# New work lists for VectorE and ScalarE, tile 13 by eight products, and the addition of x1 on GpSimd instead of in a DMA

## The reference, cut to what matters

```python
def block1(x):                       # on LN(x), _layernorm without weights
    uv = x @ in_proj_w + in_proj_b   # 512 -> 1024
    u, v = uv[..., :512], silu(uv[..., 512:])
    v = depthwise_conv3(v) + conv_b  # along the rows (time)
    h_t = a * h_{t-1} + ssm_b * v_t; y_t = ssm_c * h_t + ssm_d * v_t
    out = (u * silu(y)) @ out_proj_w + out_proj_b
    return layernorm_with_weights(out + x)

def ffn(x):                          # on LN(x1)
    h = gelu(x @ ternary(W1).T + b1) # 512 -> 2048
    return h @ ternary(W2).T + b2    # 2048 -> 512

x1  = x  + LN(block1(LN(x)))
out = x1 + LN(ffn(LN(x1)))
```

## Time and profile before

| | us |
|---|---|
| three runs: median (lowest to highest) | 1498.55 (1497.08 to 1499.59) |
| the profiled execution's own time | 1498.6 |
| its span, first to last instruction | 1496.8 |
| PE busy in the span | 1416.4 (95%) |
| DVE busy | 1220.6 (82%) |
| ACT busy | 913.1 (61%) |
| POOL busy | 356.5 (24%) |

### The profile page before, as it was taken

One profiled execution on the slowest core, in us unless ns is written; L12 is line 12 of the kernel. 1 busy time (PEld: TensorE's weight loads), 2 busy tenths in 40 slices (PEclk: granted clock), 3 DMA queues, 4 the chain that ended last, 5 costly groups with the idle time before them and its releaser, 6 DMA issues.

```text
span 1496.8 us, 25048 instructions
## 1 busy us (share of the span) xinstructions
PE 1416.4 (95%) x9002; PEld 885.7 (59%) x9002; DVE 1220.6 (82%) x2402; ACT 913.1 (61%) x1504; POOL 356.5 (24%) x522
## 2 busy tenths in 40 slices
PE   7999999899999999999999999999999999989997
PEld 4444646457475664756657566574666747555664
DVE  7999869788797887978889698897988879898634
ACT  7997756556466564674756556575665646743543
POOL 4243321222202222131222212222122220222111
PEclk9999999999999999999999999999999999999999
DMA  8702613215122151320513304142131512202320
GB/s 248 259 30 58 166 31 76 38 29 113 29 63 51 29 113 29 85 43 15 113 28 87 55 13 103 29 100 42 44 71 29 113 29 58 29 1 57 57 29 29
DMA packets 164653, 98.13 MB, mean 66 GB/s; under 512 B 133680, under 2 KB 133680, under 8 KB 164400
## 3 DMA queue, kind: packets, MB, share of 16 engines
q1 hardware_dynamic: 155888, 80.79, 21.2%
q0 software_dynamic: 8640, 15.73, 7.4%
HBM read 31.49 MB, written 32.51 MB: 43 GB/s over the span
## 4 chain that ended last, share of the span: by engine, by line
PE 37%; DVE 30%; issue 15%; ACT 8%; POOL 3%; DVEq 0%; POOLq 0%; ACTq 0%
PE f1b L614 6%; PE f1b L613 6%; DVE bn L904 5%; PE f2b L664 4%; DVE ring L922 3%; PE misc L576 3%; PE misc L578 3%; PE misc L577 3%; PE f2b L654 3%; ACT tp L1944 3%; ACT xn L1934 2%; DVE hb L1161 2%; PE f2b L639 2%; PE f2b L637 2%; POOL rsc L2278 2%
## 5 line engine op out<-in xcount | busy, mean ns | idle before, releaser
L613 PE MATMUL f1b<-x3T,w 128*128 128x256 f16 x1792 | 400.7, 274 | 0.0
L614 PE MATMUL f1b<-x3T,w 128*128 128x256 f16 x1792 | 400.5, 274 | 0.0
L1840 ACT ACTIVATE ring<-f1b,par 128x256 f32<-128x256 f32 x480 | 201.1, 470 | 237.3 <-PE f1b L614 237.0
L2277 POOL TENSOR_SCALAR ve<-mv 128x4 f32<-128x4 f32 (+2 forms) x89 | 36.8, 414 | 797.5 <-DVE mv L914 797.3
L922 DVE SCALAR_TENSOR_TENSOR ring<-ring,f_sc 128x512 f16<-128x512 f32 x256 | 187.3, 738 | 34.8 <-ACT ring L1854 34.8
L654 PE MATMUL f2b<-w,ring 128*128 128x512 fp8e5 x768 | 197.1, 379 | 0.0
L613 PEld LDWEIGHTS f1b<-x3T,w 128*128 128x128 fp8e5 x1792 | 176.2, 98 | 24.8 <-issue 0.4
L614 PEld LDWEIGHTS f1b<-x3T,w 128*128 128x128 fp8e5 x1792 | 176.0, 98 | 24.2
L1854 ACT ACTIVATE ring<-ring,f_sc 128x512 f16<-128x512 f32 x256 | 182.2, 719 | 0.0
L576 PE MATMUL misc<-x1T,win_hi 128*128 128x512 f16 x456 | 179.4, 393 | 0.0
L577 PE MATMUL misc<-x1T,win_hi 128*128 128x512 f16 x456 | 178.6, 392 | 0.0
(11 more groups left out here) (263 smaller groups left out, 2823.4 us busy)
## 6 DMA issues: line engine op xcount, KB each, us to landing
out_dram<-xs SPq DMA_DIRECT2D x60, 256.0 KB, 2.7
xs<-x_dram SPq DMA_DIRECT2D x14, 1024.0 KB, 6.1
out_dram<-hb POOLq DMA_DIRECT2D x36, 256.0 KB, 5.4
out_dram<-stage POOLq DMA_DIRECT2D x24, 256.0 KB, 4.6
ring<-w1t_dram SPq DMA_DIRECT2D x3, 1024.0 KB, 13.1
stage<-w2t_dram SPq DMA_DIRECT2D x3, 1024.0 KB, 8.4
x1T<-tp SPq DMA_TRANSPOSE x68, 3.1
xs<-x_dram SPq DMA_DIRECT2D x4, 256.0 KB, 4.1
```

Source lines behind the costliest of these rows:

```text
L613: pe.matmul(o_, w, src[:, k, h * TH:(h + 1) * TH], start=k == 0, stop=False)
L614: mm = pe.matmul(o_, w, src[:, KC + k, h * TH:(h + 1) * TH], start=False, stop=k == KC - 1)
L1840: ins = act.activation(gg[:, i % G_SLOTS, ts], f1b[i % 2][:, ts], ACT.Gelu, bias=par[:, B1 + chunk:B1 + chunk + 1], scale=1.0 / ACT_SCALE)
```

## The change

1. **Lists of VectorE and ScalarE.** In the first part of a stage: the taps of blocks 2 and 3 stand before the scans; d_conv of blocks 2 and 3 moves from 6.15 and 7.15 to 4.15 and 4.16; ffn_norm of a tile by seven moves from 4.15..5.2 to 6.15..7.2; the statistics of blocks 2 and 3 of the FFN's result (f_stats) move from .8 to 2.27; lo of the sixth unit (5) gets the time 4.2. In the written part h_add(c, 0) stands before the last t_lo, and three operations of `drain` stand between the t_lo. In the second part lo has new times (AT_LO_SECOND).
2. **combine.** Of eight, three are made in the written part of stage 3, and one instead of three at its end.
3. **Tile 13 by eight.** `seven` ends at tile 12. Stage 15's sums, seven-part drains and its statistics in two halves become lo, f_add and statistics of a tile by eight.
4. **The sum with x1.** `finish` is GpSimd's tensor_tensor of two 128 x 512 float32 blocks in SBUF. SyncE stores the result (`store`) and no longer stores x1. `load_x(e+4)` waits for fin_ok, that is for the four additions of tile e, and stands in SyncE's list behind its four stores.

```diff
-AT_TAP0, AT_TAP2 = (1.1, 1.15, 1.4, 1.45), (1.3, 1.35, 2.4, 2.45)
+AT_TAP0, AT_TAP2 = (1.1, 1.15, 1.4, 1.45), (1.3, 1.35, 2.25, 2.26)
-AT_LO = (1.2, 2.2, 2.32, 2.38, 3.36)
-AT_D_CONV, AT_CENTRE = (3.15, 3.16, 6.15, 7.15), (13.3, 13.5, 14.3, 14.5)
+AT_LO = (1.2, 2.2, 2.32, 2.38, 3.36, 4.2)
+AT_D_CONV, AT_CENTRE = (3.15, 3.16, 4.15, 4.16), (13.3, 13.5, 14.3, 14.5)
+AT_LO_SECOND = (9.3, 11.2, 11.65, 13.2, 14.2, 15.2, 16.2)
+AT_F_STATS_SEVEN = 2.27
+AT_F_NORM_SEVEN = (6.15, 6.2, 7.15, 7.2)
-AT_COMBINED = (7.65, 7.66, 11.65, 11.66, 14.65, 17.5, 17.51, 17.52)
+AT_COMBINED = (7.65, 9.25, 11.65, 14.65, 17.5)
@@
     def seven(t):
-        return 1 < t < NT - 2
+        return 1 < t < NT - 3
@@ load_x
                 if t >= X_SLOTS:
-                    sp.wait_ge(n3_ok, NB * (t - X_SLOTS + 1))
-                    for j in range(NB):
-                        sp.wait_ge(x1_st[j], 16 * (t - X_SLOTS + 1))
+                    sp.wait_ge(fin_ok, NB * (t - X_SLOTS + 1))
@@
-            def store_x1(t):
...
+            def store(t, j):
+                if t < NT - 1:
+                    sp.wait_ge(fin_ok, NB * t + j + 1)
+                else:
+                    sp.wait_ge(fin_last, j + 1)
+                sp.dma_start(out_d[t, j], fo(t, j)).then_inc(out_st[j], 16)
@@ SyncE, for each stage s
-                if e is not None and e + X_SLOTS < NT:
-                    load_x(e + X_SLOTS)
-                if s == 3:
-                    store_x1(1)
+                if e is not None:
+                    for j in range(NB):
+                        store(e, j)
+                    if e + X_SLOTS < NT:
+                        load_x(e + X_SLOTS)
@@ VectorE, the written part
+                parts = drain(fa, 0) if seven(fa) else []
                 if n is not None:
-                    for j in range(NB):
-                        t_lo("t1", n, j)
...
+                    t_lo("t1", n, 1)
+                    for part in parts[:3]:
+                        part()
+                    t_lo("t1", n, 2)
+                    h_add(c, 0)
+                    for part in parts[3:4]:
+                        part()
+                    t_lo("t1", n, 3)
+                    parts = parts[4:]
@@ GpSimd
             def finish(e, j):
                 pool.wait_ge(fn_ok, NB * e + j + 1)
-                pool.wait_ge(x1_st[j], 16 * (e + 1))
-                pool.dma_start(out_d[e, j], fo(e, j), accum_op=ALU.add).then_inc(out_st[j], 16)
+                pool.tensor_tensor(fo(e, j), fo(e, j), xs[:, e % X_SLOTS, j, :], ALU.add).then_inc(fin_ok, 1)
```

More of the change, by code:

```diff
@@ L519, in _ @@
                     transposes("t3", c)
-                if c is not None and c < NT - 1:
-                    store_x1(c)
             for j in range(NB):
-                store_last(j)
+                store(NT - 1, j)
             for j in range(NB):
-                sp.wait_ge(x1_st[j], 16 * (NT - 1))
-                sp.wait_ge(out_st[j], 16 * (NT - 1))
-                sp.wait_ge(last_st[j], 16)
+                sp.wait_ge(out_st[j], 16 * NT)
         @block.tensor
@@ L1036, in epilogue @@
                     return (spread(AT_F_ADD, .1, drain(e, 1))
-                            + spread(AT_F_STATS, .1, [lambda j=j: f_stats(e, j) for j in range(2, NB)])
-                            + spread(AT_F_AGGR, .01, [lambda j=j: aggr(4, e, j) for j in range(2, NB)]))
+                            + spread(AT_F_STATS_SEVEN, .001, [lambda j=j: f_stats(e, j) for j in range(2, NB)])
+                            + spread(AT_F_STATS_SEVEN + .004, .001, [lambda j=j: aggr(4, e, j) for j in range(2, NB)]))
                 return (spread(AT_F_ADD, .2, [lambda j=j: f_add(e, j) for j in range(NB)])
@@ L1739, in _ @@
                     gate(c, 1)
+                if s == 3:
+                    combine(2, 0)
                 if n is not None:
@@ L1751, in _ @@
                     gate_lo(c, 3)
+                parts = drain(fa, 0) if seven(fa) else []
                 if n is not None:
-                    for j in range(NB):
-                        t_lo("t1", n, j)
+                    if s == 3:
+                        combine(0, 0)
+                    t_lo("t1", n, 0)
+                    if s == 3:
+                        combine(0, 1)
+                    t_lo("t1", n, 1)
[7 more added lines that the diff above has]
+                    parts = parts[4:]
                 if s == NT - 1:
@@ L1760, in _ @@
                 if c is not None:
-                    parts = drain(fa, 0) if seven(fa) else []
                     for j in range(NB):
-                        h_add(c, j)
-                        for part in parts[2 * j:2 * j + 2]:
-                            part()
+                        if n is None or j > 0:
+                            h_add(c, j)
                         if s == NT - 1:
@@ L1773, in _ @@
                                 aggr(1, c, j - 2)
+                        for part in parts[2 * j - 2:2 * j] if j else []:
+                            part()
                     h_stats(c, NB - 1)
@@ L1783, in _ @@
                 if s == 3:
-                    works = [b2_difference] + [lambda q=q, g=g: combine(q, g) for q in range(4) for g in range(2)]
-                    items += list(zip((AT_COMBINED[0],) + AT_COMBINED, works))
+                    b2_difference()
+                    items += [(at, lambda i=i: combine(*divmod(i, 2))) for i, at in zip((2, 3, 5, 6, 7), AT_COMBINED)]
                 if s < NT - 1:
@@ L1788, in _ @@
                 if fa is not None:
-                    at_lo = AT_LO_LAST if s == NT - 1 else [j + 1.2 for j in range(half(s), FC)]
+                    at_lo = AT_LO_LAST if s == NT - 1 else AT_LO_SECOND
                     items += lows(fa, range(half(s), FC), [0] * half(s) + list(at_lo))
@@ L1804, in _ @@
                     t_lo("t3", NT - 2, 3)
-                    parts = drain(NT - 3, 1)
-                    for part in parts[:4]:
-                        part()
+                    f_add(NT - 3, 0)
+                    f_add(NT - 3, 1)
                     h_add(NT - 1, 0)
-                    for part in parts[4:]:
-                        part()
+                    f_add(NT - 3, 2)
+                    f_add(NT - 3, 3)
                     for j in range(NB):
-                        if j > 1:
-                            f_stats(NT - 3, j)
+                        f_stats(NT - 3, j)
                         if j < NB - 1:
@@ L2215, in _ @@
                 if e is not None:
-                    items += [(at, lambda j=j: ffn_norm(e, j)) for j, at in enumerate(AT_F_NORM)]
+                    items += [(at, lambda j=j: ffn_norm(e, j)) for j, at in enumerate(AT_F_NORM_SEVEN if seven(e) else AT_F_NORM)]
                 if c is not None and s < NT:
```

26 lines of the change are left out of this document (7 added, 19 removed).

## The result

| | before | after |
|---|---|---|
| median of four runs, us | 1498.87 | 1458.83 (1455.72 to 1462.79) |
| ratio, 95% interval | | 0.9736 (0.9711 to 0.9761) |
| the profiled execution: its own time, its span | 1498.6, 1496.8 | 1458.7, 1456.9 |
| PE busy | 1416.4 (95%) | 1400.7 (96%) |
| DVE busy | 1220.6 (82%) | 1263.0 (87%) |

The kernel is 40 us faster, by the profiled executions 39.9. Lines have moved by about eleven: L653 of after is L664 of before, L955 is L966, L911 is L922, L1074 is L1085 and L1130 is L1141.

What follows compares the result with a forecast made beforehand. PE, busy for 95% of the span, was taken as the bound. From 1498.6 us, eleven stages of 89.4 for 91.41 (-22), stage 15 (-8.5) and stage 4's start (-2.3) gave 1465.8, rounded to 1466 us; range 1433 to 1508.

Steps and rivals of the forecast that it cites:

- rival B: All four additions go in one by one ahead of the sums; PE waits 3.1 us, clock always falls: 1480 us, chance 0.15.
- The scan's wait: First part of a stage: with d_conv early, block 3's scan no longer waits; undisturbed, 2.31 us of PE's idle time goes.
- the margin: Sums of units 4 and 5 ready at 557.5 us, 1.5 ahead of PE, of which 1.0 was taken.
- h_add: Placed ahead of the last split, it removes PE's 1.2 us wait in a stage, with 1.0 us to spare.
- The price of an addition: On VectorE ahead of the sums of units 4 and 5: each addition costs 0 or 1.02 us.
- rivals A and C: A: additions cost nothing, 1428 to 1440 us, chance 0.27; C: additions starve, ln1 waits for x, 1500 to 1520, chance 0.17.
- How many get in: Three of four additions go in ahead of the sums of units 4 and 5, so PE waits 2.1 us.
- The clock: Behind the wait for the sums, the clock falls in ten of twelve stages, 1.69 us each.
- The stage without waits: A stage without PE's 4.12 us of waits and the 1.69 us fall would take 85.9 us.
- The end: Tile 13 by eight removes the waits for sums in stage 15: 8.5 us taken, with 0 and 9.9 as ends.
- load_x: It waits for the fourth addition; x lands at 566.3 us, wanted by ln1 at 565.9; the delay is covered.
- The DMAs: The store of x1 and the adding DMAs are gone; no wait of PE rests on them, so nothing is gained.

Runs made afterwards that it cites:

- the multiplications: After, with GpSimd multiplying the block by 1.0 in place of adding x1 in the tiles by seven: 1421.98 us.
- The kernel with three additions: After, with block 3 of the tiles by seven added over 8 of 512 columns only: 1451.82 us.
- the kernels without waits: After with the adding DMA in place of GpSimd's additions, 1415.66 us; after with all additions of tiles by seven cut to 8 columns, 1418.33 us.

## Why the prediction was right, and where it wasn't

The time (1466 predicted, 1458.8 measured) and its sign were right, and so was the mechanism: what PE waited for, what took these waits away, and that each addition delays VectorE ahead of the sums. How many additions get in was wrong, and there rival B, to which the prediction gave 0.15, had it right. That the stage came out at 89.4 us all the same is luck: over eleven stages the fourth addition cost about 10 us more than predicted, the rarer falls 5.5 and the faster stage 4.4 less. The 7 us that are left lie at the end.

*The waits and their causes.* Right. The scan's wait, the margin (1.0 taken, 0.7 to 0.8 measured), h_add (1.2, and 1.2 when it was put back), the start of stage 4 (2.3 taken, 2.4 measured). The second pair of sums had no margin to spare, as was said: without additions its products begin 1.13 us behind the start of the four matmuls ahead of them, elsewhere 0.87.

*The price of an addition.* 1.02 us from stage 15, 0.97 measured. Right, and it was the number on which all depended. The row of 6.48 us, on which rivals A and C rested, wasn't repeated: the longest of the new additions took 2.28 us.

*How many get in.* Wrong: three taken, four came. The step said that the fourth arrives when the sums are nearly through. It placed the sums where an undisturbed VectorE makes them; but three additions had pushed them back by 2.9 us, and the fourth caught the first of them. An addition makes room for the next. The count was that of rival B. The rule of the Trainium skill (page "SBUF — State Buffer", section "SBUF: two separate sides") that stood behind it agrees with these additions: all four went in one by one, and VectorE lost 0.97 us of the 1.27 of each. It doesn't agree with the multiplications, which read SBUF as well and cost VectorE 0.32 us each; there the measurement decides. The kernel with three additions shows the predicted case: a wait of 2.1 us and a fall in most stages.

*The clock.* Wrong: falls in ten of twelve stages taken (1.4 us for a stage), four of nine measured, 0.9 on the average. The price of one was not 1.69 either but 1.6 twice and 2.9 twice. I took it that a wait as long as before, in the same place, brings the fall with it. In the profiled executions it came less often with a wait of 3.0 than with one of 2.1, and in the kernel before with additions behind none of eleven waits of 2.3 us (380 to 1301 us). The largest part of rival B's miss (1480) comes from this too: it counted a fall in each stage, which is 9 of its 21 us; 7 more are the end's and 4 the faster stage's.

*The stage without waits.* 85.9 taken, 85.33 measured. Rows 1 gave the waits of PE as idle time, but PE's busy time was 85.93 there and is 85.24 in the kernels without waits: with the four waits 0.7 us of busy time went too. In after a stage less its wait is 88.52 - 3.02 = 85.5. With 3.0 for 2.1, 0.9 for 1.4 and 85.5 for 85.9 a stage comes to 89.4, the predicted figure.

*The end.* 10.5 taken (2.0 for the last of the eleven stages and 8.5 for tile 13), 17.7 measured. Tile 13 by eight is worth 11.6 alone. Left out was the wait of 1.6 us for h_add in stage 15, and the caution of 1.4 was not needed. The stage ahead of it lost 3.5 us, not 2.0: 0.6 of sums, 1.2 of h_add and 1.69 of a fall of the clock, which in after doesn't come behind the wait at its start (1177.86 us). That leaves 2.6 us, and 1.9 of them lie behind VectorE's last work, in before and in after:

```profile
1491.71 0.75 DVE L1215 SCALAR_TENSOR_TENSOR hb<-hb,rs,xs 128x512 f32<-128x512 f32 x1 [0.56 <-POOL rs L2278]
1453.67 0.75 DVE L1204 SCALAR_TENSOR_TENSOR hb<-hb,rs,xs 128x512 f32<-128x512 f32 x1 [0.55 <-POOL rs L2278]
```

From there to the end of the span, 1496.8 and 1456.9 us, it is 4.3 us in before and 2.5 in after. 0.7 us are not assigned.

*load_x.* Right: VectorE waits for x in none of these stages. Two waits in all, at the beginning (what ended L893's idle time):

```profile
  DMA xs<-x_dram: 4.8, 2
```

*The DMAs.* "Nothing" was right for the stages: they take 85.33 us with the adding DMAs and without. At the end it was 1.8 us: from VectorE's last work to the end of the span it is 4.3 to 4.4 us in five kernels with the adding DMA (before, and before with tile 13 by eight, among them) and 2.5 to 2.6 in five without (after, and before with the additions on GpSimd, among them). Its other side was missed: what costs nothing need not be removed. The prediction priced the additions against each other and not against the DMA they replace. That is worth 43 us, more than the change brings.

## What to carry to other kernels

GpSimd's elementwise work with two operands in SBUF isn't free beside a dense VectorE, however idle GpSimd is: count one addition of two 128 x 512 float32 blocks (1.27 us alone) as about 1 us of VectorE in the place where it falls, and count again after each, because the delay lets the next one in. Where VectorE's margin is under that, leave the sum to a DMA that nobody waits for. And a price for a fall of the clock isn't to be carried from one timing to another: three kernels with waits of 2.1, 3.0 and 2.3 us had it behind seven of nine, four of nine and none of eleven, and one fall cost between 1.6 and 2.9 us.

## What the runs showed of the hardware that was not expected

- VectorE and GpSimd took turns at these additions: one VectorE instruction, one addition. Scans of 1.2 us, lo of 0.7 and sums of 0.29 all lost 0.95 to 1.1 us for one addition of 1.27. One addition of a bias doesn't fit, the first of the kernel, at 106 us: it took 6.48 us in before and 6.49 in after, while VectorE's instructions of 0.72 to 0.74 us went on beside it. Why is open.
- A GpSimd multiplication by a constant over the same block cost VectorE 0.32 us, not 0.97, and took longer itself (1.5 to 2.0 us).
- The clock at equal waits. Three waits of 3.02 us, 90 us apart in the same program, were followed by a granted clock of 0.50, 0.70 and 1.00 over 5 us. Which of them is followed by a fall depends on more than the wait's length; on what, these runs leave open.
- With the adding DMAs in the kernel its span ended 4.3 us behind VectorE's last work, without them 2.5 us, though the last two stores look alike (1.64 and 1.63 us, in before and after). What takes the 1.8 us, the traces don't show.
